# Two-layer graph network on one core: the running sums go to DRAM and one gather fetches the crossing rows

## The reference

```python
# layer 0: attention over the edges of one target (8 heads of 16)
Q = V[src] @ Wq + bq;  K = V[dest] @ Wk + bk;  Vv = V[dest] @ Wv + bv
scores = einsum('ehd,ehd->eh', Q, K) / sqrt(HD) + E @ Wb + bb
alpha  = softmax of scores over the edges with the same dest
x = layernorm(x + segment_sum(alpha * Vv, dest) @ Wo + bo)

# layer 1: one softmax over ALL edges
h  = x @ W
e  = leaky_relu((h @ a1)[src] + (h @ a2)[dst])
attention = softmax(e)
x = layernorm(x + segment_sum(attention[:, None] * h[src], dst))
```

## Time and profile before

| what | value |
|---|---|
| median of 3 runs | 1279.33 us (1272.30, 1279.33, 1283.68) |
| span of the profiled execution, core 0 | 1278.0 us |
| TensorE, busy in the whole span | 729.8 us |
| VectorE, busy in the whole span | 814.2 us |
| ScalarE, busy in the whole span | 718.6 us |
| GpSimd, busy in the whole span | 760.7 us |
| first scatter of the last stage starts | 956.31 us |
| last scatter starts | 1275.39 us |
| granted TensorE clock, mean of the span | 0.776 of 2.4 GHz |

### The profile page before, as it was taken

One profiled execution on the slowest core, in us unless ns is written; L12 is line 12 of the kernel. 1 busy time (PEld: TensorE's weight loads), 2 busy tenths in 40 slices (PEclk: granted clock), 3 DMA queues, 4 the chain that ended last, 5 costly groups with the idle time before them and its releaser, 6 DMA issues.

```text
span 1278.0 us, 14643 instructions
## 1 busy us (share of the span) xinstructions
PE 729.8 (57%) x3271; PEld 477.8 (37%) x3271; DVE 814.2 (64%) x3724; ACT 718.6 (56%) x2048; POOL 760.7 (60%) x805
## 2 busy tenths in 40 slices
PE   0467777776776776777745455445436534444442
PEld 0335545544544544555544354434422111111110
DVE  5487777776776777777855456555447755565553
ACT  3358777777777777777612333334355544554443
POOL 7565666666666666663166665666625566556665
PEclk9988888778888787778956777776775777667776
DMA  7355575566765666653437667576542222122210
GB/s 211 114 175 169 172 220 166 171 216 186 222 209 179 188 190 184 182 188 115 146 98 219 220 208 226 181 235 199 190 136 75 77 70 72 57 77 67 74 55 28
DMA packets 82017, 196.96 MB, mean 154 GB/s; under 512 B 19802, under 2 KB 21993, under 8 KB 81920
## 3 DMA queue, kind: packets, MB, share of 16 engines
q1 hardware_dynamic: 56746, 148.35, 36.8%
q0 software_dynamic: 25184, 47.69, 13.1%
HBM read 122.78 MB, written 77.22 MB: 156 GB/s over the span
## 4 chain that ended last, share of the span: by engine, by line
DVE 19%; another core or an unknown queue 14%; issue 7%; PE 7%; ACT 5%; DMA 2%; POOL 1%; DVEq 1%; SPq 0%; POOLq 0%
DVE src_b L1449 5%; DVE part L1457 4%; DVE nst L1472 3%; PE psum L727 2%; ACT node_out L780 2%; DMA src_b<-src_t 1%; ACT xsT L941 1%; DVE match L1127 1%; DVE nmv L1482 1%; PE psum L733 1%; POOL out_dram L506 1%; ACT h_res L945 1%; PE psum L755 1%; DMA x1d_in<-x_all 1%
## 5 line engine op out<-in xcount | busy, mean ns | idle before, releaser
L506 POOL DMA_INDIRECT out_dram<-yb,at_last x196 | 195.8, 999 | 144.6 <-ACT yb L780 87.4
L502 POOL DMA_INDIRECT xs<-in_x,src_tab x196 | 185.1, 944 | 154.7 <-remote 71.6
L502 POOL DMA_INDIRECT xs<-x_all,row_tab x196 | 186.8, 953 | 115.1 <-issue 55.5
L502 POOL DMA_INDIRECT h_res<-in_x,dst_tab x196 | 186.9, 954 | 59.7 <-issue 59.7
L755 PE MATMUL psum<-src_b,ident_inv 128*128 128x512 f32 x90 | 74.7, 924 | 146.7 <-DVE src_b L1449 146.7
L780 ACT ACTIVATE h_res<-node_in,shift,rstd 128x128 f32<-128x128 f32 (+1 forms) x392 | 155.7, 482 | 0.3 <-DVE shift L1259 0.3
L941 ACT ACTIVATE xsT<-psum 128x512 f32<-128x512 f32 x48 | 28.6, 597 | 203.0 <-remote 161.9
L585 PE MATMUL psum<-h_res 128*128 128x512 f32 x98 | 72.8, 833 | 119.8 <-ACT h_res L787 119.7
L727 PE MATMUL psum<-w,xsT 128*128 128x129 f32 x384 | 74.8, 356 | 73.5 <-ACT xsT L941 54.7
L780 ACT ACTIVATE yb<-psum,shift,rstd 128x128 f32<-128x128 f32 x198 | 74.5, 456 | 61.5 <-DVE shift L1465 46.1
L589 PE MATMUL psum<-xsT,h_res 128*128 128x512 f32 x98 | 90.1, 1019 | 23.7 <-ACT xsT L791 22.5
(11 more groups left out here) (302 smaller groups left out, 1855.5 us busy)
## 6 DMA issues: line engine op xcount, KB each, us to landing
x1d_in<-x_all SPq DMA_DIRECT2D x98, 256.0 KB
node_in<-in_x SPq DMA_DIRECT2D x48, 512.0 KB
x_all<-h_res SPq DMA_DIRECT2D x48, 512.0 KB
out_dram<-node_out SPq DMA_DIRECT2D x48, 512.0 KB
x_all<-yb SPq DMA_DIRECT2D x49, 256.0 KB
src_b<-src_t SPq DMA_DIRECT2D x49, 256.0 KB
node_in<-x_all SPq DMA_DIRECT2D x24, 512.0 KB
h_res<-in_edge_attr SPq DMA_DIRECT2D x7, 784.0 KB
```

The costliest lines, as they stand in the source:

```text
L502: return pool.indirect_dma_start(out=to, out_offset=None, in_=table, in_offset=bass.IndirectOffsetOnAxis(ap=idx, axis=0))
L506: return pool.indirect_dma_start(out=table, out_offset=bass.IndirectOffsetOnAxis(ap=idx, axis=0), in_=rows, in_offset=None, bounds_check=l ...
```

## The change

1. **The sums are stored.** A new DRAM tensor `agg_rows` takes the running sums of every group: SyncE issues `store_sums(g)`, 256 KB, 49 times, behind the load of `x1d_in` for group g + 4. `agg` gets five slots (`NA = 5`) in place of two, and `running(g, 0)` waits until the store and TensorE's use of group g - 5 are done.
2. **One gather takes the place of `kept`.** The 196 steps of line 1457 with their waits go. For each partition the row number of its one row is computed in the first stage (eight small VectorE instructions and one more GpSimd `iota`), and GpSimd gathers 128 rows of `agg_rows` into `part` once, in front of the last group's four scatters, when all stores have landed. The factors `fold_p` and `part_scale` go into one factor `part_mul` (two small instructions in the last stage).
3. **Orders.** VectorE's spread order starts at group 3 instead of 9, and `running(2, 0)`, `running(2, 1)` move ahead of `moments(1)`. ScalarE weighs s + 2 at the head of iteration s in place of s + 3 at its end; only `weigh(3)` changes its place among the others.
4. **Small things.** A scatter's bound is loaded into a register once instead of by a MOVE in front of each; some semaphores are merged or left out; SyncE waits for `last_x1` (the last gather of the stage before) once before it loads `x1d_in` in the scatter stage.

```diff
     XS, XD, XDT, YB, NI, NX, NO, SB, XI = 4, 8, 2, 4, 3, 3, 2, 7, 4
+    NA = 5
...
+    agg_rows = nc.dram_tensor("agg_rows", (P * TILES, D), fp32).ap()
...
-        xa, agg = src_b[:, 0:2, :], src_b[:, 2:4, :]
+        xa, agg = src_b[:, 0:2, :], src_b[:, 2:2 + NA, :]
...
+            def store_sums(g):
+                sp.wait_ge(r_chain, (g + 1) * G)
+                sp.dma_start(edge_group(agg_rows, g), agg[:, g % NA, :]).then_inc(agg_stored[g % NA], 16)
...
                 wait(sp, e_y, g - XI)
                 load_x1d(sp, g, x1d_back)
+                if g >= XI:
+                    store_sums(g - XI)
+            for g in range(GROUPS - XI, GROUPS):
+                store_sums(g)
...
+            last_node = pool.to_reg(N - 1)
+
+            def scatter(table, rows, idx):
                 return pool.indirect_dma_start(out=table, out_offset=bass.IndirectOffsetOnAxis(ap=idx, axis=0),
-                                               in_=rows, in_offset=None, bounds_check=limit - 1, oob_is_err=False)
+                                               in_=rows, in_offset=None, bounds_check=last_node, oob_is_err=False)
...
             for g in range(GROUPS):
+                if g == END:
+                    ring_done(pool, agg_stored, GROUPS, 1)
+                    gather(part[:, :], agg_rows, part_idx[:, 0:1]).then_inc(part_got, 16)
...
             for s in range(1, GROUPS):
+                if edge(s + 2):
+                    weigh(s + 2)
                 act.wait_ge(e_var, s)
...
-                if s == 1:
-                    weigh(3)
-                if edge(s + 3):
-                    weigh(s + 3)
...
+                if t == 0 and g >= NA:
+                    dve.wait_ge(agg_stored[g % NA], use(g - NA, NA) * 16)
+                    wait(dve, e_y, g - NA)
...
-            def kept(g, t):
-                if g == BASE and t == 0:
-                    dve.wait_ge(own_chain, g * G)
-                    c.link(v.tensor_scalar(part[:, :], part[:, :], fold_p[:, :], None, ALU.mult))
-                wait(dve, own_chain, g * G + t)
-                v.scalar_tensor_tensor(part[:, :], tile(agg[:, g % 2, :], t), first_last[:, g * G + t:g * G + t + 1],
-                                       part[:, :], ALU.mult, ALU.add).then_inc(own_chain, 1)
-
-            def sums_free(s):
-                if s > 1:
-                    wait(dve, e_y, s - 2)
-                    dve.wait_ge(own_chain, (s - 1) * G)
...
+            running(2, 0)
+            running(2, 1)
             moments(1)
             aggregates(1)
-            for t in range(G):
-                kept(0, t)
...
+            running(2, 2)
+            shift_of(1)
+            running(2, 3)
+
+            for s in range(3, GROUPS + 2):
                 if edge(s):
-                    sums_free(s)
                     running(s, 0)
...
-                if edge(s):
-                    kept(s, 0)
-                if edge(s - 1):
                     aggregates(s - 1)
-                if edge(s):
-                    for t in range(1, G):
-                        kept(s, t)
...
             dve.wait_ge(f_pe, 2)
-            v.scalar_tensor_tensor(total[:, :], part[:, :], part_scale[:, :], bank[5][:, 0:P], ALU.mult, ALU.add).then_inc(f_dve, 1)
+            dve.wait_ge(part_got, 16)
+            v.scalar_tensor_tensor(total[:, :], part[:, :], part_mul, bank[5][:, 0:P], ALU.mult, ALU.add).then_inc(f_dve, 1)
```

More of the change, by code:

```diff
@@ L229, in gnn_kernel @@
         part = sb("part", [P, D])
+        part_base = sb("part_base", [P, 1], i32)
+        part_idx = sb("part_idx", [P, 1], i32)
+        part_f = sb("part_f", [P, 6])
+        part_place, part_row, part_lead, part_tail, part_mul, part_any = (part_f[:, i:i + 1] for i in range(6))
         last_xT = match[:, :, :].rearrange("p t w -> p (t w)")[:, 0:GW]
@@ L498, in _ @@
                                base=HD - 1, pattern=[[HD, H]], channel_multiplier=-1)
+            pool.iota(part_base[:, :], pattern=[[1, 1]], base=0, channel_multiplier=TILES)
             pool.iota(place_i[:, :], pattern=[[1, ROW]], base=1, channel_multiplier=0).then_inc(built, 1)
@@ L558, in _ @@
                         pool.wait_ge(e_applied, g)
-                    scatter(out, N, tile(yb[:, g % YB, :], t), idx).then_inc(e_scat[g % YB], 16)
+                    scatter(out, tile(yb[:, g % YB, :], t), idx).then_inc(e_scat[g % YB], 16)
             pool.wait_ge(f_act, 3)
-            scatter(out, N, total[:, :], carry_idx[:, 1:2]).then_inc(f_scat, 16)
+            scatter(out, total[:, :], carry_idx[:, 1:2]).then_inc(f_scat, 16)
         @block.tensor
@@ L818, in out_half @@
                     act.wait_ge(out_stored[o % NO], out_count(o - NO))
-                scale_rows(node_out[0:n, o % NO, :], node_x1[0:n, k % NX, :], n, HALVES[half], ratio[:, k, :], None)\
-                    .then_inc(out_applied, 1)
+                scale_rows(node_out[0:n, o % NO, :], node_x1[0:n, k % NX, :], n, HALVES[half], ratio[:, k, :], None)
             def queries(g):
@@ L964, in _ @@
             fn(fold_p[:, :], lead_min, ACT.Exp, bias=min_p[:, :], scale=-1.0).then_inc(exp_done, 1)
-            act.wait_ge(min_b, 1)
+            act.wait_ge(spread_pe, 2)
             fn(fall_p[:, :], bank[3][:, 0:1], ACT.Exp, bias=max_p[:, :]).then_inc(fall_done_p, 1)
@@ L1026, in _ @@
             v.memset(sum_row[:, 0:1], 0.0)
-            v.memset(part[:, :], 0.0)
             v.memset(carryT[:, 0:1], 0.0)
@@ L1098, in tables @@
                 v.tensor_copy(at_last[:, :], last_f[:, :])
+                v.tensor_tensor_reduce(out=match[:, 0, 0:TILES], in0=first_last[:, :], in1=place[:, 0:TILES], scale=1.0, scalar=0.0,
+                                       op0=ALU.mult, op1=ALU.add, accum_out=part_place)
+                v.tensor_copy(part_any, part_base[:, :])
                 v.tensor_tensor(carry_f[:, 6:7], carry_f[:, 5:6], dst_f[:, 0:1], ALU.add)
@@ L1104, in tables @@
                 c.link(v.tensor_tensor(ends_diff[:, 0:ROW], ends_f[:, :], ends_prev[:, :], ALU.subtract))
+                v.tensor_scalar(part_tail, part_place, float(BASE * G), None, ALU.is_gt)
+                v.tensor_scalar(part_lead, part_place, 0.0, None, ALU.is_gt)
+                v.tensor_scalar(part_row, part_place, 1.0, -1.0, ALU.max, ALU.add)
                 v.memset(ends_diff[0:1, ROW:ROW + 1], 0.0)
@@ L1555, in _ @@
             c.link(v.tensor_tensor(part_scale[:, :], fall_p[:, :], inv_sum[:, :], ALU.mult))
+            v.tensor_tensor(part_mul, part_tail, part_scale[:, :], ALU.mult)
+            running(2, 0)
+            running(2, 1)
             moments(1)
             aggregates(1)
[L1558 to L1585 removed]
+            running(2, 2)
+            shift_of(1)
+            running(2, 3)
+            for s in range(3, GROUPS + 2):
                 if edge(s):
[L1587 removed]
                     running(s, 0)
[L1589 removed]
+                if s - 2 > 1:
                     shift_of(s - 2)
```

81 lines of the change are left out of this document (32 added, 49 removed).

## The result

The changed kernel takes **1260.53 us** (median of six runs, 1257.93 to 1266.55) against 1278.51 of the kernel before in the six runs beside them; the ratio is 0.987, 95% interval [0.984, 0.990]. The forecast was 1261 us. The interval excludes no change, and 1.3% is more than the 1% that the prediction took as its border.

A forecast was written before the change was run, and what follows sets the result against it. GpSimd's scatter pace and its waits for `yb` bound the last stage: 198 x 1.299 = 257.2 plus 44.5 of gaps gives 301.7 against 320.1, -18.4; 1278.0 - 18.4 + 1.3 gives 1261 us, range 1228 to 1285.

The forecast's parts named there:

- The 196 steps: `kept` on VectorE in the scatter stage: removing them shortens groups, so bursts hold more groups and fewer gaps remain.
- F = 3.5: ScalarE's time per group in us in the scatter stage's fast stretch, down from 4.0 by 0.5 to 0.6.
- S, 9.4 to 12.9: Time per slow group in us: 9.4 if holds leave with the removed instructions, 12.9 if each keeps its length.
- rival B: Scatter stage: the slow stretch lets one group through whatever its work, so bursts stay; 1273 or 1279 us, chance 0.21.
- k = 4.9: Groups per burst of scatters if slow groups keep 12.9 us; 5.5 was taken, and 4.9 gave 1267 us.
- The start of the hold: When, within a GpSimd scatter burst, other engines' semaphore waits grow: some 8.6 us after the burst begins.
- The gaps' number and length: GpSimd's waits for `yb` between bursts: 7.7 of 5.4 us plus 2.9 for the first, 44.5 us.
- VectorE's start: Start of the scatter stage: group 1 scaled some 1.6 us earlier, first gap 2.9 us instead of 4.83.
- The stores at nothing: SyncE's 49 stores of 256 KB in the scatter stage were counted as costing nothing.
- rival C: Scatter stage: the stores' packets bring the hold on sooner, 5.6 us instead of 8.6; about 1292 us, chance 0.13.
- The port rule: VectorE with two SBUF inputs and GpSimd lock each other out; some 2 us less by the rule, nothing taken.
- Rival A: Scatter stage: holds mainly `kept`'s own chain, so GpSimd is the bound without them; 1223 to 1244 us, chance 0.25.

The follow-up runs named there:

- run 5: Changed kernel with the old chain added back from group 3 on, four dependent 128x128 additions per group on VectorE: 1275.77 us, ratio 0.999.
- run 7: Kernel before without the 196 steps and their waits, two slots and old orders, no stores and no gather: 1263.97 us, ratio 0.990.
- run 2: Changed kernel with four 128x128 VectorE additions per group from group 3 on, without waits on one another or semaphores of their own: 1260.12 us, ratio 0.985.
- run 1: Changed kernel without the 49 stores, the gather and its wait: 1254.63 us, ratio 0.982.

## Why the prediction was right

The number was right, and so was its main cause. But that 301.7 lies so near to 301.1 is partly luck: several terms were off, and they cancelled.

- **What bounds the stage** was right: GpSimd at 1.29 us a scatter and its waits for `yb`. 198 scatters at 0.993 + 0.30 are 256.0 us of the 301.1; the forecast had 257.2 and 44.5 of gaps.
- **The 196 steps are the main term:** 14.0 us of stage by adding them back (run 5), 15.7 by taking them out of the kernel before (run 7), of the 19.0. The forecast's model of how they cost, a longer group and so fewer groups in each burst at a fixed gap, is not borne out: with work alone (run 2) bursts are 16 again and the time stays, because the gap shrinks to 4.1. Their own busy time, 58.1 us in the earlier trace rows, is no measure: put back without its chain, it costs 0.7.
- **F = 3.5** was too long: 3.3 us. The whole wait for the shift went (0.85 to 0.23), not 0.5 to 0.6 us of it.
- **S, 9.4 to 12.9, was wrong.** The slow group did not get shorter with the steps taken out of it, and did not keep its 13.6 us either: it takes 14.2 to 15.5, as long as the burst lasts. One group a burst gets through at that speed, with a second one stretched to about 5.5. That is the mechanism of rival B, k = 1 + fast groups. With the measured 3.3 its formula gives 4.6, and the forecast's own, with 3.3 and 14.8, gives 4.9; k is 5, so the count doesn't tell the two apart. It is nearly the forecast's lower end, k = 4.9, which it priced at 1267.
- **The start of the hold** was given as 8.6 us into a burst and came at 10.5 or later, with and without the stores.
- **The gaps' number and length** cancelled: 2.9 and 7.7 of 5.4 were forecast, 44.5 us; it was 2.86 and nine of 4.0 to 5.6, together 47.4 us, of which 44.4 go beyond the usual 0.30. The forecast counted whole gaps on top of a 0.30 that each scatter already had; for 8.7 gaps that is 2.6 us twice.
- **VectorE's start** was right: moments(1) wait 1.18 us, the first gap is 2.86 against 2.9 forecast. But orders and slots were counted with this 1.9 us only; in the absence of the steps they are worth 9.1 by the stages of run 7 and run 1.
- **The stores at nothing** was probably too low: run 1 has 5.8 us for them and the gather, of which the forecast had 1.3. The rule of the Trainium skill ("DMA: Bandwidth & Descriptors", section "SWDGE vs HWDGE vs iDMA"), that each DMA engine takes turns between the queues, pointed that way. Yet the hold came no sooner, the bursts were 20 with and without stores, and rival C's mechanism did not occur. Whether and how the stores lengthen the gaps by 0.5 us was not tried.
- **The port rule** of the Trainium skill ("SBUF — State Buffer", section "SBUF: two separate sides"): the scatters' mean went from 999 to 993 ns, 1.2 us for 196 of them, and back to 1000 with the work of run 2; the shortest and the median barely moved (980 and 982 before, 982 and 985 after). This agrees with the small price that the trace had left the rule.
- **Rival A** would have needed holds that are `kept`'s own; run 7 has them without `kept`.

## What to carry to other kernels

Where an engine issues DMAs back to back and the others feed it, look at when their waits grow, not only at how busy they are: a stretch in which the same instructions suddenly wait microseconds for their own semaphores is worth a pause of 2 us in the issuing engine before it is worth a rewrite. The best version here is the changed kernel with that pause in front of every third group (0.978 [0.972, 0.983]), and about two thirds of its gain, 1.4 of 2.2%, are to be had without the rest of the change. What an instruction costs is what it and its waits do together to the loop that repeats; busy time put back without its chain cost almost nothing here.

## What the runs showed of the hardware

- While GpSimd issues indirect DMAs without a pause, steps from one instruction to a waiting one on the other engines grow from 0.2 us or less: with the change up to 5.9 us from VectorE to itself, 5.2 from VectorE to ScalarE and 1.7 from VectorE to TensorE. It begins some 8.6 us into the burst before the change and from 10.5 us on with it (about 20 where the engines are paced), and ends 2 to 3 us after GpSimd stops. A pause of 2.0 to 3.4 us for the landing of the scatters, after every 8 or 12 of them, kept this away in the changed kernel but for one step of 3.1 us; after every 16 it did not.
- 256 KB stores beside scatters raised the DMA share from 0.23 to 0.36 and left the length of GpSimd's scatters as it was (mean 993 ns with them, 990 without, run 1).
- What in the chip holds the steps, and why work and chain together cost 14.0 us where each alone costs 0.7 and 2.6, stays open. More pauses on other loops (the gathers of the stage before show the same hold) were not tried.
